# Expert stage of a Perceiver block: weight copies made two tiles ahead, up products in one PSUM bank, outputs in two

## The reference, cut to what matters

```
x = x + cross_attention(layernorm(x), ctx, ctx)      # 32 batches, 32 queries, 257 keys, 16 heads of 8
x = x + gated_mix(layernorm(x))                      # six 128x128 products, one sigmoid gate
x = x + experts(layernorm(x))                        # 1024 tokens, 8 experts, 2 per token

# experts, E = 8, D = 128, F = 512
logits = x @ gate_kernel; weights, selected = top_k(logits, 2); weights = softmax(weights)
tokens are sorted by expert (2048 rows); for each row t of expert e:
    layer_1 = t @ w0[e]            # 128 -> 512, the "gate" product
    layer_2 = t @ w1[e]            # 128 -> 512, the "up" product
    out     = (silu(layer_1) * layer_2) @ wo[e]      # 512 -> 128
rows go back to their tokens, times their weight, and a token's two rows are added
```

## Time and profile before

| | us |
|---|---|
| median of 3 runs | 255.34 |
| lowest and highest | 254.56, 256.04 |
| profiled execution, first to last instruction (span) | 253.1 |
| expert stage in it, first gather's issue to the last product of placed rows | 162.6 to 247.2 |
| of it PE busy, 165.5 to 228.0 | 55.24 of 62.50 |

### The profile page before, as it was taken

How to read it: one execution, slowest core, us unless ns; L and a number is a source line. 1 busy time by engine, 2 the same in 40 slices (tenths; PEclk the granted TensorE clock), 3 DMA queues, 4 the chain that set the end, 5 groups by cost and what they waited for, 6 DMA issues and landing times.

```text
span 253.1 us, 6393 instructions
## 1 busy us (share of the span) xinstructions
PE 218.9 (86%) x2107; PEld 176.8 (70%) x2107; DVE 153.7 (61%) x501; ACT 138.1 (55%) x420; POOL 122.9 (49%) x258
## 2 busy tenths in 40 slices
PE   6889999999999999997589971679988989899980
PEld 6667877777777777775345750368878878888970
DVE  2688878686868787775174668434543544436822
ACT  2389878798998979898124132024444443334400
POOL 2744663646374735434434132664555656564403
PEclk9799999999999999999979995599999999999998
DMA  6696050422329000000000007021111111112052
GB/s 196 237 341 219 5 198 11 130 80 78 135 41 313 24 4 4 0 4 0 3 0 1 3 0 169 0 57 29 22 42 32 38 40 43 39 30 39 13 166 85
DMA packets 12609, 18.17 MB, mean 72 GB/s; under 512 B 1823, under 2 KB 8227, under 8 KB 12578
## 3 DMA queue, kind: packets, MB, share of 16 engines
q1 hardware_dynamic: 10738, 14.64, 18.1%
q0 software_dynamic: 1408, 2.58, 4.6%
q10 hardware_dynamic: 432, 0.54, 0.6%
HBM read 14.07 MB, written 4.01 MB: 71 GB/s over the span
## 4 chain that ended last, share of the span: by engine, by line
PE 65%; DVE 12%; DMA 5%; another core or an unknown queue 5%; issue 4%; POOL 4%; DVEq 1%; ACT 1%; POOLq 1%; SPq 0%; ACTq 0%
PE bank L752 11%; PE bank L905 11%; PE bank L742 9%; PE bank L724 8%; PE bank L782 7%; PE bank L915 6%; PE bank L726 6%; DMA pt_sb<-planes 2%; PE bank L759 2%; DMA vec_sb<-vectors 1%; DVE stats L969 1%; POOL row_in_tile L523 1%; PE bank L833 1%; DVEq L1223 1%
## 5 line engine op out<-in xcount | busy, mean ns | idle before, releaser
L602 ACT ACTIVATE p_sb<-bank,neg_max 128x257 f32<-128x257 f32 x128 | 59.0, 474 | 17.1 <-DVE neg_max L1044 17.1
L905 PE MATMUL bank<-slot_ft,w_now 128*128 128x128 f32 x368 | 48.0, 277 | 5.1 <-issue 4.7
L1044 DVE TENSOR_REDUCE neg_max<-bank 128x1 f32<-128x257 f32 x128 | 46.6, 418 | 6.8 <-PE bank L742 6.4
L905 PEld LDWEIGHTS bank<-slot_ft,w_now 128*128 128x128 f32 x368 | 44.6, 192 | 6.7 <-issue 6.1
L611 ACT ACTIVATE pt_sb<-bank 128x512 f32<-128x512 f32 x64 | 35.0, 611 | 0.3 <-PE bank L752 0.3
L536 POOL DMA_INDIRECT planes<-y_sb,y_row x21 | 21.3, 1012 | 27.1 <-DVE slot_meta L1219 19.8
L752 PE MATMUL bank<-ident,p_sb 128*128 128x128 f32 x256 | 33.3, 273 | 0.8 <-ACT pt_sb L611 0.8
L456 POOL TENSOR_TENSOR o_half<-o_masked 128x64 f32<-128x64 f32 x32 | 10.2, 318 | 48.9 <-DVE o_masked L1073 48.9
L1265 DVE TENSOR_TENSOR hid_ft<-silu_sb,bank 128x512 f32<-128x512 f32 x23 | 15.8, 686 | 28.9 <-remote 16.2
L653 ACT ACTIVATE slot_ft<-bank 128x128 f32<-128x128 f32 x23 | 6.4, 277 | 43.7 <-PE bank L894 38.3
L752 PEld LDWEIGHTS bank<-ident,p_sb 128*128 128x128 f32 x256 | 28.9, 141 | 1.4 <-ACT p_sb L602 1.0
(11 more groups left out here) (179 smaller groups left out, 319.1 us busy)
## 6 DMA issues: line engine op xcount, KB each, us to landing
w_sb<-w SPq DMA_DIRECT2D x8, 512.0 KB, 4.7
ctx_sb<-ctx_keys SPq DMA_DIRECT2D x7, 512.0 KB, 4.0
wo_sb<-wo SPq DMA_DIRECT2D x8, 256.0 KB, 5.0
table<-rows_tok SPq DMA_DIRECT2D x2, 520.0 KB
planes<-zero_rows SPq DMA_DIRECT2D x2, 512.0 KB, 7.9
pt_sb<-planes SPq DMA_DIRECT2D x4, 256.0 KB, 4.8
out<-norm_tok SPq DMA_DIRECT2D x2, 256.0 KB, 2.3
x_tok<-x SPq DMA_DIRECT2D x1, 448.0 KB, 4.9
```

Of the source, the lines that this page charges most:

```text
L602: act.activation(p_sb[b % 2][:, g, :], s_bank[g][:, 0:SKV], ACT.Exp, bias=neg_max[b % 2][:, g:g + 1], accum_out=sum_last[:, 0, b, g:g + 1] ...
L905: last = pe.matmul(bank[2 * m + s % 2][:, tile(c)], w01_now[s % 2][:, m, tile(c)], slot_ft[s % 2][:], start=True, stop=True)
L1044: dve.tensor_reduce(neg_max[b % 2][:, g:g + 1], s_bank[g][:, 0:SKV], AX.X, ALU.max, negate=True).then_inc(max_ready, 1)
```

## The change

Seven edits, all in the expert stage:

- `w01_now` has three buffers (`NOW_BUFS`). They lie in the context buffers of the attention stage, which are idle by then.
- ACT's and DVE's weight copies are for tile s+2 and no longer for s+1. The first two are made ahead of the loop.
- ACT's order in the loop is silu(s), slot_features(s+1), gate_weights(s+2); it was slot_features(s+1), silu(s), gate_weights(s+1).
- DVE's order is product(s), up_weights(s+2), weigh_output(s-1), keep_meta(s+1); it was keep_meta(s+1), up_weights(s+1), product(s), weigh_output(s-1).
- Experts' numbers are loaded four tiles at a time (`AT_ONCE`), without the bounds check.
- All up products go to bank 2. The up product of tile s therefore waits for DVE's product of tile s-1.
- Outputs alternate between banks 5 and 3. project(s) therefore waits for the weighing of tile s-2 and not of s-1.

```diff
-        w01_now = [sb(f"w01_now{n}", [128, 2, F]) for n in range(2)]
+        w01_now = [ctx_sb[n][:].rearrange("p (m k) c -> p m (k c)", m=2) for n in range(NOW_BUFS)]
+        y_bank = (bank[5], bank[3])
...
@@ ScalarE
             def gate_weights(s):
-                expert = act.value_load(tile_expert[0:1, s:s + 1], min_val=0, max_val=E - 1)
-                if s >= 2:
-                    act.wait_ge(gate_half_done, s - 1)
+                if s >= NOW_BUFS:
+                    act.wait_ge(gate_half_done, s - NOW_BUFS + 1)
...
+            load_experts(0)
             gate_weights(0)
             slot_features(0)
+            gate_weights(1)
             for s in range(SLOT_TILES):
-                if s + 1 < SLOT_TILES:
-                    slot_features(s + 1)
                 act.wait_ge(gate_half_done, s + 1)
                 if s >= 2:
                     act.wait_ge(hid_ready, s - 1)
                 act.activation(silu_sb[s % 2][:], bank[s % 2][:], ACT.Silu).then_inc(silu_ready, 1)
                 if s + 1 < SLOT_TILES:
-                    gate_weights(s + 1)
+                    slot_features(s + 1)
+                if s + 2 < SLOT_TILES:
+                    if (s + 2) % AT_ONCE == 0:
+                        load_experts(s + 2)
+                    gate_weights(s + 2)
@@ TensorE
-                if s >= 2:
-                    pe.wait_ge((silu_ready, hid_ready)[m], s - 1)
+                if m == 0 and s >= 2:
+                    pe.wait_ge(silu_ready, s - 1)
+                if m == 1 and s >= 1:
+                    pe.wait_ge(hid_ready, s)
+                to = bank[2] if m else bank[s % 2]
...
                 pe.wait_ge(hid_ready, s + 1)
-                if s >= 1:
-                    pe.wait_ge(y_ready, s)
+                if s >= 2:
+                    pe.wait_ge(y_ready, s - 1)
...
+            def load_experts(s):
+                many = range(s, min(s + AT_ONCE, SLOT_TILES))
+                _, values = nc.values_load_multi_w_load_instructions(
+                    tile_expert[0:1, many.start:many.stop], engines=[mybir.EngineType.PE], min_val=0, max_val=E - 1,
+                    skip_runtime_bounds_check_because="a sum of ones and zeros, cut to the last expert by the minimum")
+                expert.update(zip(many, values))
@@ VectorE
             for s in range(SLOT_TILES):
-                if s + 1 < SLOT_TILES:
-                    keep_meta(s + 1)
-                    up_weights(s + 1)
                 dve.wait_ge(silu_ready, s + 1)
                 dve.wait_ge(up_half_done, s + 1)
...
-                dve.tensor_tensor(hid_ft[s % 2][:].rearrange("p c r -> p (c r)"), silu_sb[s % 2][:], bank[2 + s % 2][:],
+                dve.tensor_tensor(hid_ft[s % 2][:].rearrange("p c r -> p (c r)"), silu_sb[s % 2][:], bank[2][:],
                                   ALU.mult).then_inc(hid_ready, 1)
+                if s + 2 < SLOT_TILES:
+                    if (s + 2) % AT_ONCE == 0:
+                        load_experts(s + 2)
+                    up_weights(s + 2)
                 if s >= 1:
                     weigh_output(s - 1)
+                if s + 1 < SLOT_TILES:
+                    keep_meta(s + 1)
```

More of the change, by code:

```diff
@@ L53 @@
 Y_BUFS = 4
+NOW_BUFS = 3
+AT_ONCE = 4
 LATE = 2
@@ L665, in _ @@
             act.wait_ge(tile_expert_ready, 1)
+            expert = {}
+            def load_experts(s):
+                many = range(s, min(s + AT_ONCE, SLOT_TILES))
+                _, values = nc.values_load_multi_w_load_instructions(
+                    tile_expert[0:1, many.start:many.stop], engines=[mybir.EngineType.Activation], min_val=0, max_val=E - 1,
+                    skip_runtime_bounds_check_because="a sum of ones and zeros, cut to the last expert by the minimum")
+                expert.update(zip(many, values))
+            load_experts(0)
             gate_weights(0)
             slot_features(0)
+            gate_weights(1)
             for s in range(SLOT_TILES):
-                if s + 1 < SLOT_TILES:
-                    slot_features(s + 1)
                 act.wait_ge(gate_half_done, s + 1)
@@ L900, in half_hidden @@
                 pe.wait_ge((gate_w_ready, up_w_ready)[m], s + 1)
-                if s >= 2:
-                    pe.wait_ge((silu_ready, hid_ready)[m], s - 1)
+                if m == 0 and s >= 2:
[3 more added lines that the diff above has]
+                to = bank[2] if m else bank[s % 2]
                 for c in range(FC):
-                    last = pe.matmul(bank[2 * m + s % 2][:, tile(c)], w01_now[s % 2][:, m, tile(c)], slot_ft[s % 2][:],
+                    last = pe.matmul(to[:, tile(c)], w01_now[s % NOW_BUFS][:, m, tile(c)], slot_ft[s % 2][:],
                                      start=True, stop=True)
@@ L911, in project @@
                 pe.wait_ge(hid_ready, s + 1)
-                if s >= 1:
-                    pe.wait_ge(y_ready, s)
+                if s >= 2:
+                    pe.wait_ge(y_ready, s - 1)
                 for c in range(FC):
-                    last = pe.matmul(bank[5][:, 0:D], hid_ft[s % 2][:, c, :],
+                    last = pe.matmul(y_bank[s % 2][:, 0:D], hid_ft[s % 2][:, c, :],
                                      wo_sb[:, bass.ds(expert[s], 1), c, :].rearrange("p e d -> p (e d)"),
@@ L932, in _, with load_experts @@
             expert = {}
-            def load_expert(s):
-                expert[s] = pe.value_load(tile_expert[0:1, s:s + 1], min_val=0, max_val=E - 1)
-            load_expert(0)
+            def load_experts(s):
+                many = range(s, min(s + AT_ONCE, SLOT_TILES))
+                _, values = nc.values_load_multi_w_load_instructions(
+                    tile_expert[0:1, many.start:many.stop], engines=[mybir.EngineType.PE], min_val=0, max_val=E - 1,
+                    skip_runtime_bounds_check_because="a sum of ones and zeros, cut to the last expert by the minimum")
+                expert.update(zip(many, values))
+            load_experts(0)
             turn_slots(0)
@@ L942, in _ @@
                 half_hidden(s, 0)
-                if s + 1 < SLOT_TILES:
-                    load_expert(s + 1)
+                if s + 1 < SLOT_TILES and (s + 1) % AT_ONCE == 0:
+                    load_experts(s + 1)
                 if s + 1 < SLOT_TILES:
@@ L1221, in up_weights @@
             def up_weights(s):
-                expert = dve.value_load(tile_expert[0:1, s:s + 1], min_val=0, max_val=E - 1)
-                if s >= 2:
-                    dve.wait_ge(up_half_done, s - 1)
-                dve.tensor_copy(w01_now[s % 2][:, 1, :], w01_sb[:, bass.ds(expert, 1), 1, :].rearrange("p e f -> p (e f)")
+                if s >= NOW_BUFS:
+                    dve.wait_ge(up_half_done, s - NOW_BUFS + 1)
+                dve.tensor_copy(w01_now[s % NOW_BUFS][:, 1, :], w01_sb[:, bass.ds(expert[s], 1), 1, :].rearrange("p e f -> p (e f)")
                                 ).then_inc(up_w_ready, 1)
@@ L1247, in weigh_output @@
                     dve.tensor_copy(y_row[s % Y_BUFS][:], slot_meta[:, s, 1:2])
-                dve.tensor_scalar(y_sb[s % Y_BUFS][:], bank[5][:, 0:D], slot_meta[:, s, 0:1], None,
+                dve.tensor_scalar(y_sb[s % Y_BUFS][:], y_bank[s % 2][:, 0:D], slot_meta[:, s, 0:1], None,
                                   ALU.mult).then_inc(y_ready, 1)
@@ L1252, in _, with load_experts @@
             dve.wait_ge(tile_expert_ready, 1)
+            expert = {}
+            def load_experts(s):
+                many = range(s, min(s + AT_ONCE, SLOT_TILES))
+                _, values = nc.values_load_multi_w_load_instructions(
+                    tile_expert[0:1, many.start:many.stop], engines=[mybir.EngineType.DVE], min_val=0, max_val=E - 1,
+                    skip_runtime_bounds_check_because="a sum of ones and zeros, cut to the last expert by the minimum")
+                expert.update(zip(many, values))
+            load_experts(0)
             up_weights(0)
             keep_meta(0)
+            up_weights(1)
             for s in range(SLOT_TILES):
-                if s + 1 < SLOT_TILES:
-                    keep_meta(s + 1)
-                    up_weights(s + 1)
                 dve.wait_ge(silu_ready, s + 1)
```

3 lines of the change are left out of this document (2 added, 1 removed).

## The result

The changed kernel takes 254.33 us (median of 20 runs, 251.81 to 261.17), the kernel before 255.31 us (20 runs, 253.19 to 256.82). The ratio is 0.9952, with an interval of 0.9928 to 0.9975: faster by 0.5%, where 1.2% was forecast. The fastest and the slowest run of the changed kernel lie 9.4 us apart, those of the kernel before 3.6. The profiled execution has a span of 252.6 us instead of 253.1.

The account below looks back on a forecast made before the run. The pace was taken to be a loop through TensorE, DVE and POOL, whose indirect DMAs hold TensorE's completions. POOL's idle time 2.8 less and the start 0.3 gave 255.3 - 3.1 = 252.2 us, range 247.8 to 257.6.

Parts of the forecast that it names:

- R: Moment in the expert loop when TensorE's held-back completions arrive, about 5.7 us behind the start of POOL's run of four issues.
- the two waits: TensorE's idle time, 4.7 us ahead of gate and up products, 2.7 us ahead of the projection; counts only if the loop shortens.
- the loads: Experts' numbers in registers: 23 loads become 6; a load of four takes 0.30 to 4 x 0.30 us; gain taken as 0.
- the kind of cycle: Whether a two-tile cycle of the loop is long or short: one long first and seven short were forecast.
- short cycle: Two-tile cycle where DVE's product and copy are over before R; POOL idle for 1.5 us ahead of its run.
- C: Rival, expert loop: copy ahead of the weighing makes all cycles long, 260.2 us; with milder forms, chance 0.20.
- long cycles: Two-tile cycles where DVE's product waits until R; POOL's idle time ahead of the run forecast at 2.65 us.
- the sum's main term: POOL's idle time ahead of the loop's eight runs: from 16.0 to 13.2 us, 2.8 less.
- the start: Ahead of POOL's first run: silu(1) and gate(1) wait less, so that run starts 0.3 us earlier.
- one short cycle so brings on the next: Loop step: after a short cycle signals come early enough to be seen at once, giving seven short cycles with 1.51 us idle.
- rival A: The loop breaks: POOL never stops and TensorE bounds, 6.9 us less, 248.4 us; chance 0.17.
- copy ahead of the weighing: DVE's copy between product and weighing adds about 0.48 us in a long cycle, nothing in a short one.

Follow-up runs that it names:

- e1: The kernel before without scatters and without the gathers beyond the sixth: 243.28 us, ratio 0.9573 to the kernel before.
- e6: The changed kernel with each scatter replaced by a POOL memset of about 1.0 us: 243.27 us, ratio 0.9511 to the kernel before.
- e2: The changed kernel without scatters and without the gathers beyond the sixth: 242.93 us, ratio 0.9529 to the kernel before.
- e4: The changed kernel without the scatters of outputs, gathers kept: 243.33 us, ratio 0.9524 to the kernel before.
- e3: The kernel before without the scatters of outputs, gathers kept: 242.32 us, ratio 0.9533 to the kernel before.
- e13: The changed kernel unchanged, run once more: 253.42 us, ratio 0.9911 to the kernel before.
- e16: The changed kernel with the experts' numbers loaded one at a time: 251.82 us, ratio 0.9838 to the kernel before.
- e14: The changed kernel with the old banks (two up, one output) and DVE's weighing ahead of its copy: 250.73 us, ratio 0.9851 to the kernel before.
- e18: The changed kernel with the old banks, DVE's weighing ahead of its copy, and single loads: 252.8 us, ratio 0.9863 to the kernel before.
- e17: The changed kernel with single loads, a second time: median 253.89 us of six runs, ratio 0.9794 to the kernel before (from three of them).
- e10: The changed kernel with the old banks (two up, one output): 253.2 us, ratio 0.99 to the kernel before.
- e11: The changed kernel with one gate bank and two up banks: median 255.96 us of six runs, ratio 0.9899 to the kernel before (from three).
- e9: The changed kernel with DVE weighing the output and keeping the tile's rows ahead of its copy: 254.35 us, ratio 0.9945 to the kernel before.
- e12: The changed kernel with a POOL memset of about 0.5 us behind each gather in the loop: 253.5 us, ratio 0.9896 to the kernel before.
- e8: The changed kernel with an even tile's scatter also waiting for the next tile's projection: 257.65 us, ratio 1.0057 to the kernel before.

## Why the prediction was wrong

**Right: what bounds the stage.** TensorE's finished signals are held by POOL's indirect DMAs: e1 to e6 show it. The loop R, product, weighing, scatter, three issues sets the pace; without it the kernel takes 11 to 12 us less.

**Right: the two waits, the loads, the kind of cycle.** The gate copy's and `y_sb`'s waits went, and gave nothing by themselves (e2 and e4 beside e1 and e3). A load of four is 0.34 us, near the lower end of its bounds (one line of DVE's register loads, after: ns least, median, most), where one number took 0.30:

```profile
L1282 DVEq TENSOR_LOAD <-tile_expert x6: 341/344/750, 162.6 to 228.2; - x6
```

The Trainium skill (DMA: Bandwidth & Descriptors, "Latency and other measured facts") has about 600 ns as the floor of a load; no warm load in these traces comes near it. The same section of the Trainium skill says that the compiler unrolls by four to amortize it. Reading four at once does save sequencer time here, 23 x 0.30 down to 6 x 0.34 us, but no run became faster by it.

The short cycle was forecast at 4.9 + 1.51 = 6.41 us and measured at 6.39 to 6.45, and a short cycle did bring on the next, as long as no run of six came. C's long cycles did not come, but for one (2.48 us ahead of 212.45).

**Wrong: the sum's main term, 2.8 us off POOL's idle time.** Terms of the profiled execution, forecast and measured: the start -0.3, measured +0.5 (first scatter 173.85 to 174.37); the loop up to tile 16's scatter -2.8, measured -1.7 (55.17 to 53.51); from there to the end 0, measured +0.6 (24.08 to 24.72). In all -3.1, measured -0.5. In the run medians it is -1.0. e13, the same kernel, has +0.1, -0.9 (54.32) and -0.4 (23.64), in all -1.2. So of what is missing against the forecast the loop holds 1.1 of 2.6 us in the first profile, and all of the 1.9 in the second. The end varies from 23.2 to 24.9 us between the profiles of all kernels with scatters in the loop, and nothing shows that the change moves it.

The step that failed is the one that follows the short cycle: "one short cycle so brings on the next", taken for all seven that follow the first. The earlier product also lets a third output be ready before the fourth issue ends. I had this path as rival A, and priced it at a gain of 6.9 us, on the ground that POOL would never stop and TensorE would bound. Its own objection, that "completions would have to be seen between back-to-back issues", was the fact: while POOL did not stop, nothing that TensorE finished after 191 us was seen until 195.73. The term that it needed: from 187.18 to 205.08 five tiles took 17.9 us, where at 3.20 each they would have taken 16.0, so 1.9 us lost, with 2.93 us of idle TensorE and the slow clock behind it. Another 1.0 us went in the long cycle from 205.08 to 212.45. Without such a run the forecast's number can come: e16's span is 249.7 against 250.0 forecast. It need not: e14 and e18 have 250.8 and 250.5, e17 251.7 and e10, with two long cycles, 252.5. That runs of six are what keeps the changed kernel from the forecast is seen in its two profiles; in its other runs it is likely, and not shown.

**Wrong: what A is worth.** I read 7.3 us of idle TensorE in 62.5 from the earlier trace rows. Eight products show as 1.06 us but follow each other every 0.89 (190.65 and 191.55 in e6), and each break in the row hides 0.17 us of that in the busy time. By e6's 2.79 us a tile, 10.5 us were there in 16 tiles.

**Wrong: the start.** In the changed kernel the granted clock rose at 169.85 us, in the kernel before at 165.6 us, so the first gate product took 2.07 us instead of 1.16. The late rise stands in the profiles of after, e2, e4, e11, e14 and e17, the early one in those of before and the other thirteen experiments, ten of which carry the change or most of it (e13 is the changed kernel itself). So the change alone doesn't set it; whether it makes it likelier is open. Nor does the forecast 0.3 us show where the rise is early: from the first gather to the first scatter e13 takes 11.31 us, the kernel before 11.24.

**Half right: copy ahead of the weighing.** With two output banks it makes no difference (e9). With one it may: e14 has 0.9851 and e10 0.99, with intervals that overlap, and TensorE's wait for `y_sb` is 4.4 us instead of 7.4.

## What to carry to other kernels

Where a wait is removed inside a loop that runs through several engines, work out what the earlier signal lets the other engines join up, not only the case in which it arrives in its usual place; the gain and its reversal lay 0.4 us apart here. A wait that costs 7 us in the table can cost nothing, and may be worth having if it keeps a worse pattern from forming. And count what could be gained from the spacing of an undisturbed row of products, not from busy time.

## What the runs showed of the hardware

- GpSimd's indirect DMAs hold back the semaphore updates of TensorE. In the loop two every 2.5 to 3.0 us do, gathers as well as scatters, mostly until about 1 us behind the last (5.9 us of ACT's wait in the run of six). One every 2.8 us does not, with a memset of 1.0 us beside it or without. Not shown: by which path.
- Some updates come through late in the middle of a run: in the profile after, the up product that ended at 189.56 was seen at 190.76, when the third issue was about to end.
- In the loop the first issue of a run held nothing, and the hold began about 0.3 us into the second. Gate products that ended 0.35 us (after, 182.43) and 0.32 us (e13, 182.01) into it were seen 0.03 us behind; two that ended 0.30 and 0.31 us into it (e16, 181.97 and 188.40) were seen 0.44 us late. Other places differ: 0.80 us into a second issue in e12 (205.80) nothing was held, nor during the first five gathers ahead of the loop.
- After 2.93 us of idle TensorE the granted clock was 0.5 (1.2 GHz) for 3.4 us; after 1.43 and 0.34 us close together (e12, ahead of 211.91 and 213.51 us) as well. After 0.82 and 0.34 us (e12, ahead of 181.79 and 183.39 us) it stayed at 1.00, and behind e8's seven waits of 0.80 to 0.93 us it stayed at 1.00.
